# A new order of steps in the local attention's turn and in the four joins between stages

## What is computed

```python
x = layernorm(x + attn(x))        # 16 heads of 16, causal over 512, softmax, w_out
x = layernorm(x + ffn(x))         # "ffn" is two layers of the following

def _layer(x, wqkv, qs, ksc, wo, lg, lb, w1, b1, w2, b2):
    h = shift_token(x)            # half of the channels one token late
    q, k, v = split(h @ wqkv)     # 8 heads of 64
    q, k = rotary_xpos(l2norm(q) * qs, l2norm(k) * ksc)
    o = local_attention(q, k, v)  # blocks of 128 see themselves and the block before
    x = x + o @ wo
    h = layernorm(shift_token(x)) * lg + lb
    a, g = split(h @ w1 + b1)     # 2 x 682
    return x + (a * gelu(g)) @ w2 + b2
```

## Time and profile before

| | |
|---|---|
| median of 3 runs | 1863.88 us (1859.23 to 1865.08) |
| the profiled execution, own time | 1865.3 us |
| its span, first to last instruction | 1863.8 us |
| mean granted TensorE clock | 0.95 of full speed |
| busy: PE | 1744.8 us, 94% |
| busy: DVE | 1144.1 us, 61% |
| busy: ACT | 1008.8 us, 54% |
| busy: POOL | 863.7 us, 46% |

### The profile page before, as it was taken

One profiled execution on the slowest core, in us unless ns is written; L12 is line 12 of the kernel. 1 busy time (PEld: TensorE's weight loads), 2 busy tenths in 40 slices (PEclk: granted clock), 3 DMA queues, 4 the chain that ended last, 5 costly groups with the idle time before them and its releaser, 6 DMA issues.

```text
span 1863.8 us, 42583 instructions
## 1 busy us (share of the span) xinstructions
PE 1744.8 (94%) x13984; PEld 1321.1 (71%) x13984; DVE 1144.1 (61%) x2853; ACT 1008.8 (54%) x1927; POOL 863.7 (46%) x886
## 2 busy tenths in 40 slices
PE   5899999999869999999998999789999999989997
PEld 3566656666447777777777888667777777768886
DVE  5477666676667676667643333766667667535554
ACT  2565566655626555556563555445556555554543
POOL 3233343333345655566642333545566655444544
PEclk7799889998879999999999999989999999999999
DMA  4433434323110011100022212201001110212221
GB/s 140 142 123 96 136 116 133 116 88 124 48 46 13 34 34 34 34 0 33 23 81 91 67 57 80 69 12 35 34 0 34 34 34 23 81 57 90 79 90 46
DMA packets 105656, 121.29 MB, mean 65 GB/s; under 512 B 23386, under 2 KB 78340, under 8 KB 105604
## 3 DMA queue, kind: packets, MB, share of 16 engines
q1 hardware_dynamic: 99412, 98.08, 16.9%
q0 software_dynamic: 6192, 22.55, 3.4%
HBM read 82.55 MB, written 37.77 MB: 65 GB/s over the span
## 4 chain that ended last, share of the span: by engine, by line
PE 69%; DVE 13%; ACT 6%; issue 6%; POOL 2%; SPq 2%; DMA 1%; DVEq 0%; ACTq 0%; POOLq 0%
PE b L1210 6%; PE b L704 4%; PE b L1235 4%; PE d L1151 4%; PE d L1104 3%; PE b L676 3%; PE d L1106 3%; PE d L1105 3%; DVE l_t L1057 3%; DVE d L1077 3%; PE d L1623 2%; PE d L1625 2%; PE d L1624 2%; PE b L1623 2%; PE b L1624 2%
## 5 line engine op out<-in xcount | busy, mean ns | idle before, releaser
L491 DVE TENSOR_REDUCE a_negm<-d 128x2 f32<-128x256 f32 (+3 forms) x256 | 201.4, 815 | 127.5 <-PE d L637 125.6
L454 ACT ACTIVATE a_PT<-b 128x384 f32<-128x384 f32 (+1 forms) x384 | 184.9, 524 | 137.8 <-PE b L676 71.1
L907 POOL TENSOR_TENSOR l_t<-l_t,l_t 128x512 f32<-128x512 f32 x128 | 165.5, 1293 | 149.5 <-DVE l_t L1059 148.4
L1077 DVE CUSTOM_DVE_ANT_0 d<-d,window 128x256 f32<-128x256 f32 (+1 forms) x512 | 184.6, 423 | 29.2 <-PE d L1176 29.0
L1476 POOL TENSOR_TENSOR m_hid_lo<-m_hid,m_hid_hi 128x512 fp32r<-128x512 f32 x80 | 105.0, 1322 | 153.1 <-ACT m_hid_hi L1537 152.9
L991 ACT ACTIVATE l_PT<-b 128x512 f32<-128x512 f32 (+1 forms) x256 | 125.4, 542 | 83.6 <-PE b L1218 80.3
L1104 PE MATMUL d<-w,l_xt 128*128 128x512 f32 x384 | 166.6, 434 | 3.2 <-DVE l_t L1059 2.3
L1105 PE MATMUL d<-w,l_xt 128*128 128x512 f32 x384 | 152.6, 397 | 0.0
L1106 PE MATMUL d<-w,l_xt 128*128 128x512 f32 x384 | 152.0, 396 | 0.0
L1210 PE MATMUL b<-l_Q,l_K 64*128 64x256 f32 x1536 | 138.8, 293 | 4.4 <-ACT l_PT L991 4.4
L1210 PEld LDWEIGHTS b<-l_Q,l_K 64*128 64x128 f32 x1536 | 108.1, 185 | 44.3 <-issue 28.4
(11 more groups left out here) (222 smaller groups left out, 4924.0 us busy)
## 6 DMA issues: line engine op xcount, KB each, us to landing
a_Q<-qk_parts SPq DMA_DIRECT2D x192, 64.0 KB, 2.1
a_K<-qk_parts SPq DMA_DIRECT2D x192, 64.0 KB, 2.1
qk_parts<-a_qk_hi SPq DMA_DIRECT2D x32, 256.0 KB, 2.1
qk_parts<-a_qk_lo SPq DMA_DIRECT2D x32, 256.0 KB, 2.1
xin<-after_attn SPq DMA_DIRECT2D x32, 256.0 KB, 3.0
m_xr<-after_attn SPq DMA_DIRECT2D x16, 512.0 KB, 4.0
after_attn<-rows_out POOLq DMA_DIRECT2D x14, 512.0 KB, 5.5
xin<-in_L_attn_x SPq DMA_DIRECT2D x8, 512.0 KB, 3.4
```

The source lines that it names most:

```text
L454: nc.scalar.activation(PT[:, p // PG % 2, 2 * (p % PG) + hh, QOFF[t]:QOFF[t] + nq], SC[hh][:, 0:nq], ACT.Exp, scale=AD ** -0.5).then_inc(e ...
L491: dve.tensor_reduce(negm[:, q, 2 * p:2 * p + 2], MX[i % 2][:, :, 0:nk], AX.X, ALU.max, negate=True).then_inc(max_done, 1)
L907: pool.tensor_tensor(t1[:, par, w, :], t1[:, par, w, :], t2[:, par, w, :], ALU.add)\
L1077: m = dve.tensor_tensor_reduce(out=o, in0=o, in1=mask, scale=-1.0, scalar=-NEG, op0=ALU.add, op1=ALU.min, accum_out=negm[:, q + t, p // 2, ...
```

## The change

Only lists of steps change: the turn of the local attention (both layers use it) and the first four joins. Each list holds the same steps as before; the turns of the first attention and of the feed-forward and the last join stay as they were. No instruction is added, removed or altered; each engine issues its own in a new order, DMAs included.

```diff
--- before.py
+++ after.py
@@ -842,11 +842,11 @@
 
 
     STEPS = parse("""
-        f_x:0 f_xe:0 st:0 sm:4 f_qk:0 f_qe:0 st:1 f_qk:1 ps:0 f_qe:1 f_iv:0 f_qk:2 sm:5 f_qe:2 st:2 f_qk:3
-        f_qe:3 sm:6 pv:0 f_qk:4 f_iv:1 f_qe:4 f_qk:5 f_qe:5 sm:7 sv:0 z:0 st:3 f_qk:6 ps:1 f_iv:2 f_qe:6 zn:0
-        mt:1 f_qk:7 f_qe:7 st:4 f_iv:3 pv:1 st:5 ps:2 sv:1 z:1 st:6 zn:1 f_t:0 f_te:0 zs:0 pv:2 sv:2 f_sm:0
-        f_t:1 zs:1 z:2 f_te:1 st:7 zn:2 f_sm:1 f_t:2 pv:3 f_te:2 f_sm:2 ps:3 f_t:3 sv:3 f_te:3 f_sm:3 xr:0 zs:2
-        z:3 f_v:0 zn:3 zs:3 f_v:1 f_v:2 f_mt:0 f_v:3 out:0 out:1 out:2 out:3""")
+        f_x:0 f_xe:0 sm:4 st:0 f_qk:0 f_qe:0 f_qe:1 f_qk:1 st:1 sm:5 ps:0 f_qk:2 f_iv:0 f_qe:2 ps:1 st:2
+        f_qe:3 f_qk:3 st:3 sm:6 f_iv:1 f_qe:4 f_qk:4 f_qk:5 sm:7 f_qe:5 z:0 f_iv:2 zn:0 pv:0 sv:0 f_qk:6
+        f_qe:6 mt:1 f_qe:7 f_qk:7 st:4 f_iv:3 pv:1 st:5 ps:2 z:1 sv:1 st:6 f_t:0 zn:1 pv:2 f_te:0 z:2 sv:2
+        f_sm:0 f_te:1 f_t:1 zn:2 ps:3 st:7 f_sm:1 f_t:2 zs:0 pv:3 f_te:2 f_sm:2 zs:1 zs:2 f_te:3 f_t:3 sv:3
+        f_sm:3 z:3 xr:0 f_v:0 zn:3 zs:3 f_v:1 f_mt:0 f_v:2 out:0 out:1 out:2 f_v:3 out:3""")
     FIRST = [s for s in STEPS if s[0][0] == "f"]
 
     def sync(sp):
@@ -1712,27 +1712,29 @@
 
 JOINS = [
     parse("""
-        nx:0 +rl:0 sm:27 st:8 mt:2 st:9 pv:0 st:10 sm:28 ns:0 sm:29 st:11 sm:30 st:12 ns:1 ms:2 sm:31 +edge:0 z0:0 st:13
-        xr:0 st:14 mt:3 +f_x:0 ms:3 z1:0 pv:1 +f_xe:0 st:15 st:16 +rot:0 +f_qk:0 st:17 +f_qe:0 ms:4 st:18 +f_qk:1 st:19
-        +f_qe:1 z2:0 st:20 +f_iv:0 st:21 +f_qk:2 ms:5 z0:1 st:22 +f_qe:2 z1:1 z3:0 st:23 +f_qk:3 pv:2 +f_qe:3 ms:6 z2:1
-        +f_iv:1 ms:7 z0:2 z1:2 +f_qk:4 pv:3 +f_qe:4 z0:3 z3:1 +f_qk:5 z2:2 z1:3 z3:2 z2:3 +f_qe:5 +f_iv:2 z3:3 +f_qk:6
-        nwo:0 out:0 +f_qe:6 out:1 +f_qk:7 out:2 out:3 +f_qe:7 +f_iv:3 end:0 +pick:0 +set:0 ns:2 +f_t:0 +f_te:0 +f_sm:0
-        +f_t:1 +f_te:1 +f_sm:1 +f_t:2 +f_te:2 +f_sm:2 +f_t:3 +f_te:3 +f_sm:3 +f_v:0 +f_v:1 +f_v:2 +f_mt:0 +f_v:3
-        +banks:0"""),
+        st:8 mt:2 sm:27 st:9 sm:28 sm:29 ms:2 ns:0 ns:1 st:10 pv:0 sm:30 +rl:0 st:11 st:12 ms:3 sm:31 st:13
+        nx:0 z0:0 st:14 xr:0 z1:0 mt:3 +edge:0 st:15 +f_xe:0 ms:4 +f_x:0 z2:0 z0:1 st:16 +rot:0 pv:1 z1:1
+        st:17 st:18 +f_qe:0 +f_qk:0 ms:5 st:19 z3:0 +f_qk:1 +f_qe:1 st:20 +f_iv:0 ms:6 +f_qe:2 ms:7 +f_qk:2
+        z2:1 st:21 +f_qe:3 +f_qk:3 st:22 pv:2 z0:2 z1:2 +f_iv:1 st:23 +f_qe:4 +f_qk:4 +f_qe:5 z0:3 +f_qk:5
+        z3:1 z2:2 +f_iv:2 pv:3 +f_qk:6 z1:3 +f_qk:7 +f_qe:6 z3:2 z2:3 +f_qe:7 out:0 +set:0 out:1 z3:3 out:2
+        +f_iv:3 +f_te:0 +f_t:0 out:3 +f_te:1 +f_t:1 +f_sm:0 +f_t:2 +f_te:2 +f_sm:1 +pick:0 +f_t:3 end:0 nwo:0
+        +f_te:3 +f_sm:2 +f_v:0 +f_v:1 +f_v:2 +f_sm:3 ns:2 +f_v:3 +banks:0 +f_mt:0"""),
     parse("""
-        nx:0 nz:0 xr:0 nw:0 st:0 sm:4 +f_n:0 st:1 ps:0 sm:5 st:2 sm:6 pv:0 +f_m:0 sm:7 sv:0 z:0 st:3 ps:1 zn:0 mt:1 +f_t:0 st:4
-        +f_te:0 pv:1 st:5 ps:2 sv:1 z:1 nm:0 st:6 zn:1 zs:0 ns:0 pv:2 sv:2 zs:1 z:2 st:7 zn:2 pv:3 ps:3 +set:0 sv:3
-        zs:2 ns:1 z:3 zn:3 zs:3 +f_w1:0 +f_w1:1 ns:2 out:0 out:1 out:2 out:3 +f_h:0 +f_h:1 +banks:0 +nw:0"""),
+        sm:4 ps:0 nz:0 nx:0 st:0 xr:0 sm:5 +f_n:0 st:1 ps:1 sm:6 st:2 sm:7 ns:0 pv:0 z:0 sv:0 st:3 nw:0 zn:0
+        mt:1 st:4 pv:1 zs:0 ns:1 st:5 nm:0 z:1 sv:1 ps:2 +f_m:0 ps:3 st:6 zs:1 zn:1 pv:2 z:2 sv:2 zn:2 st:7
+        +f_t:0 zs:2 +f_te:0 pv:3 z:3 zs:3 sv:3 zn:3 +f_w1:0 +set:0 out:0 out:1 out:2 out:3 ns:2 +f_h:0
+        +banks:0 +nw:0 +f_w1:1 +f_h:1"""),
     parse("""
-        nx:0 +rl:0 w1:2 +edge:0 h:2 ns:0 w2:0 w1:3 ns:1 +f_x:0 +f_xe:0 w2:1 +rot:0 w1:4 h:3 +f_qk:0 h:4 xr:0 +f_qe:0 w1:5
-        +f_qk:1 +tab:0 +f_qe:1 w2:2 h:5 +f_iv:0 +f_qk:2 w2:3 +f_qe:2 +f_qk:3 w2:4 +f_qe:3 +f_iv:1 w2:5 +f_qk:4 nwo:0 y:0
-        +f_qe:4 fin:0 +f_qk:5 +f_qe:5 +f_iv:2 ns:2 +pick:0 +set:0 +f_qk:6 +f_qe:6 +f_qk:7 +f_qe:7 +f_iv:3 +f_t:0 +f_te:0
-        +f_sm:0 +f_t:1 +f_te:1 +f_sm:1 +f_t:2 +f_te:2 +f_sm:2 +f_t:3 +f_te:3 +f_sm:3 +f_v:0 +f_v:1 +f_v:2 +f_mt:0 +f_v:3
-        +banks:0"""),
+        +rot:0 ns:0 +rl:0 +edge:0 w1:2 nx:0 ns:1 h:2 w1:3 +f_xe:0 h:3 +f_x:0 w1:4 w1:5 +f_qk:0 +f_qk:1 h:4
+        +f_qe:0 +tab:0 xr:0 +f_qe:1 +f_iv:0 +f_qe:2 +f_qe:3 fin:0 w2:0 +f_iv:1 +f_qe:4 +f_qe:5 +f_qk:2 +f_qk:3
+        w2:1 +f_qk:4 +f_qk:5 +f_qk:6 +f_qk:7 +f_iv:2 +f_qe:6 w2:2 w2:3 +f_qe:7 h:5 w2:4 w2:5 +f_iv:3 +f_t:0
+        +f_t:1 +set:0 +f_te:0 y:0 +f_sm:0 +f_te:1 +f_sm:1 +f_t:2 nwo:0 +f_te:2 +f_sm:2 +f_te:3 +pick:0
+        +banks:0 +f_t:3 +f_sm:3 +f_v:0 +f_v:1 ns:2 +f_v:2 +f_v:3 +f_mt:0"""),
     parse("""
-        nx:0 nz:0 xr:0 nw:0 st:0 sm:4 +f_n:0 st:1 ps:0 sm:5 st:2 sm:6 pv:0 +f_m:0 sm:7 sv:0 z:0 st:3 ps:1 zn:0 mt:1 +f_t:0 st:4
-        +f_te:0 pv:1 st:5 ps:2 sv:1 z:1 nm:0 st:6 zn:1 zs:0 ns:0 pv:2 sv:2 zs:1 z:2 st:7 zn:2 pv:3 ps:3 +set:0 sv:3
-        zs:2 ns:1 z:3 zn:3 zs:3 +f_w1:0 +f_w1:1 ns:2 out:0 out:1 out:2 out:3 +f_h:0 +f_h:1 +banks:0"""),
+        nx:0 sm:4 st:0 +f_n:0 st:1 sm:5 nz:0 ns:0 ps:0 pv:0 sm:6 st:2 sv:0 sm:7 z:0 ps:1 st:3 ps:2 mt:1 zs:0
+        +f_m:0 ps:3 pv:1 st:4 nm:0 st:5 zn:0 z:1 sv:1 st:6 pv:2 zn:1 zs:1 ns:1 sv:2 z:2 st:7 zn:2 +f_t:0 nw:0
+        zs:2 +f_te:0 pv:3 sv:3 xr:0 z:3 zs:3 zn:3 +f_w1:0 out:0 out:1 out:2 out:3 +set:0 ns:2 +banks:0 +f_h:0
+        +f_w1:1 +f_h:1"""),
     parse("""w1:2 h:2 w2:0 w1:3 w2:1 w1:4 h:3 h:4 xr:0 w1:5 w2:2 h:5 w2:3 w2:4 w2:5 y:0 fin:0"""),
 ]
 
```

## The result

The changed kernel takes 1815.72 us (median of 4 runs, 1813.77 to 1822.56) where the kernel before takes 1862.61 beside it (4 runs, 1859.23 to 1865.08): a ratio of 0.9757, 95% interval 0.9741 to 0.9774. The forecast was 1818.0. The sum is right. Its terms are not all right: the turn gave more than I said, the pairs of joins 1 and 3 gave less, and the reason I gave for the turn does not stand by itself.

What follows compares the result with a forecast made beforehand. PE, busy 94% of the span, fills the local turn; the joins hold waits and half-clock time. Terms 8.4 + 17 + 11 + 5 + 4 = 45.4 us off the 1863.8 us span give 1818 us; range 1808 to 1845.

Steps and rivals of the forecast that it cites:

- A: Local turn loses what the joins give: one microsecond per turn makes 14 us, total 1841 us; chance 0.14.
- B: Joins give half, since an order that frees POOL makes DVE the bound there; total 1837 us; chance 0.16.
- C: Local turn: POOL's ps:1 waits for st:3's exponentials every turn; at 3.5 us per turn, 1876 us; chance 0.04.
- D: Whole kernel: nothing changes, each wait being replaced by another of its length; 1864 us; chance 0.02.
- E: Joins run at full clock and give more than 55 us; total 1805 us; chance 0.04.
- The turn: Local turn, 14 times: mt:1's stall goes (0.5 us), better neighbours 0.1; 8.4 us in all.
- covers that had to hold: Local turn: f_iv:3 ends 0.3 us before f_t:0, ps:1 arrives 1.2 us after st:3's exponentials, out:0 has 0.2 us.
- Join 0: Join 0: f_t:0 comes 16 us earlier, 1 us less behind it; 17 us, bounds 10 and 20.
- My chain: Join 0: f_t:0 late through POOL's f_qe:5, f_qk:5, pv:3 (idle 4.62 us), ms:7 behind f_iv:1; DVE idle 6.52 us.
- Join 2: Join 2: first rotation 4.3 us earlier, chain behind it 5.8 shorter, clock 2, rot:0's cost 1.1; 11 us, bounds 6 and 13.
- Joins 1 and 3: Both joins with their first feed-forward turns: out:0 to out:3 ahead of ns:2; 5 us (bounds 2, 7) and 4 (1, 6).
- nothing if so, 2 us if not: Join 1: cost of ns:0 ahead of z:0 and st:3 on ACT; nothing if its data land sooner, 2 us if not.

## Why the prediction was right, and which terms were not

**The method held, and luck made the sum closer than its terms.** The sum was made of windows whose waits could be followed, and it came out 2.6 us from the measured difference of the spans. But the turns and join 0 gave 5.9 us more than I said, and join 2, the two pairs and the stage ahead 8.5 us less; these cancel by chance. Rivals A, B, C, D and E are refuted by the windows: the turns gained, and the joins gave 32.1 us of 37. No term left its bounds except join 3's, and that one only against the execution in the earlier trace rows. (In rival B I had DVE's work wrong by a little: after 500.54 it is 40.2 us of 62.0, not 38 of 56.)

**The turn (-8.4 forecast, -11.8 measured): a mis-sized term.** The wait at mt:1 gave its 0.5 us. I put 0.1 us on better neighbours; in a turn of layer 0 it was 0.4 (0.89 in all). Most of it shows only as PE's busy time falling from 54.42 to 53.87, so a look at idle time alone can't find it. The reason beside it was incomplete: I gave the gain to sm:7's move and treated the rest as covers that had to hold. The runs say that sm:7's move alone costs 0.8 us a turn and that it needs other moves beside it; by the rows these are st:3's, ps:1's and pv:0's, and f_qk:1's early place is not enough. My walk for POOL was of the whole order, and its cover of 0.3 us ahead of f_t:0 came out at 0.38. The danger that I named, ps:1 waiting for st:3's exponentials, is a real one: 4.7 us a turn when ps:1 moves without st:3.

**Join 0 (-17, -19.5): right, and the size partly chance.** f_t:0 came 16.8 us sooner where I had 16, and the rest of the join 2.7 us shorter where I took 1. Inside it two errors cancel: DVE's first rotation came 2.9 us sooner and not 1, and POOL idles 4.1 us and not 2. The old list measures 87.4 to 91.35 us in seven kernels, the new one 67.9 or 71.9 in four. At the same mean clock of 0.83 that is 16 us less; shortest against shortest, or longest against longest, it is 19.5. My chain was a true account of the waits in it and a poor one of their worth: undone one after another they gave 3.0, 0.4 and 2.7 us.

**Join 2 (-11, -10.1): right.** Against the 62.5 us that the old list takes in the eight other kernels that have it, the gain is 9.1. The rotations start 4.3 us sooner, as forecast, and f_t:0 9.7 us. The 2 us that I put on the stretch behind f_t:0 for the clock are 0.4: it takes 18.6 us and took 19.0, and the join's mean clock is still 0.90. The cost that I took off for rot:0 is there: one DVE operation takes 1.39 us at 1144.47 beside a POOL subtraction of 1.40 that began 0.16 us ahead, and its twin at 1143.73 takes 0.28. The trace agrees with the Trainium skill (SBUF — State Buffer, Who interferes with whom), by which the one that comes second is blocked until the first is done.

**Joins 1 and 3 (-5 and -4, -2.5 and 0.0): the step that failed** is the sentence "nothing if so, 2 us if not". I let the weights land before ACT came to ns:0 because nz:0 behind ps:0 would hold the next transfers back. They still took 10.1 us from issue in join 1 and 8.7 in join 3, and ACT waited 3.2 and 3.1 us with ready work behind it. In join 1 nearly all of the loss is this (ns:0 moved: 3.4 of the 3.9 us above its old middle with the new end). In join 3 it is about a third (1.6 of 4.5 us), and there the gain of moving ns:0 is the clock's, not idle time; the rest is other waits of its new middle, which I had no term for. The ends did what was said: on the old middles they give 3.85 us in join 1 and 2.3 in join 3 inside the join, and 2.3 and 2.2 in the turns behind them, 10.6 in all where I had 9 for both pairs. Part of join 3's +2.2 is the clock: its old list takes 44.84 us at full clock, as in the earlier trace rows, and 46.2 to 47.3 in the kernels above where it has some microseconds at half clock, as the changed one has. With the turn behind it that is 73.5 to 74.5 us in eight kernels, where the changed kernel takes 71.9; so the 0.0 is set against a short execution of the old join 3, and against those eight the pair gains 1.6 us or more.

## What to carry to other kernels

A wait that is named is worth what the next latest thing on its path leaves of it, so take a chain apart link by link before giving each link a price: undoing the longest wait of join 0 brought its step 8 us forward and the end 3. In an order that was found as a whole, a step's place may pay only together with another's; ps:1, whose early place is part of an order that gains 12 us, cost 66 when it moved without the step that feeds it. Put the conversion of data that is still being loaded behind everything that is ready, on each of the engines that share in it.

## What the runs showed of the chip that I had not expected

The same join 0, instruction for instruction, took 91.35 us at a mean clock of 0.78 in one profile and 87.78 at 0.83 in another (old list), and 71.87 at 0.83 and 67.86 at 0.90 (new list): 3.6 and 4.0 us, as much as the effect of most edits here. In these stretches PE waits often and briefly and the granted clock goes between its two levels, 2.4 and 1.2 GHz; when it falls differs between executions, though the program ahead of join 0 is the same in all these kernels. The join starts between 467.7 and 473.9 us; what decides where the clock falls is not shown. Most of the difference stands at the join's head. DVE's first rotation starts at +29.3 us or about +27 with the old list, and at +26.4 or +22.4 with the new one. The rows are of the new list; the join starts at 472.26 in the changed kernel and at 470.23 in the one with the old middles of joins 1 and 3:

```profile
498.71 0.69 DVE L1054 TENSOR_REDUCE l_ss<-l_sq 128x8 f32<-128x512 f32 x1 [1.13 <-ACT l_sq L954]
```

```profile
492.65 0.69 DVE L1054 TENSOR_REDUCE l_ss<-l_sq 128x8 f32<-128x512 f32 x1 [0.51 <-ACT l_sq L954]
```

So a join of that kind should be compared at the same mean clock, or over several kernels that share its list.
